# Scores, maxima and exponentials by pairs of heads, and decay factors computed up to four steps ahead, in a decoder layer with a selective scan

## The reference, cut to what matters

```python
# 1: causal attention, 16 heads of 16
scores = einsum('bhqd,bhkd->bhqk', Q, K) / sqrt(16)
attn = softmax(where(causal, scores, -inf), axis=-1)
out = einsum('bhqk,bhkd->bhqd', attn, V)
x = layernorm(x + out.reshape(b, s, 256) @ Wo.T)
# 2: selective scan over ctx, 256 channels, 16 states; x is the gate
def step(state, xs):
    d_t, B_t, C_t, u_t = xs
    dA = exp(d_t[..., None] * A)
    state = state * dA + (d_t * u_t)[..., None] * B_t[:, None, :]
    y_t = einsum('ben,bn->be', state, C_t)
x = layernorm(x + swapaxes((y + D * u) * silu(x), 1, 2))
# 3: mixture of 8 experts, the best 2 for each row
x = layernorm(x + sum_e w_e * (silu(0.5 * x @ w_gate[e]) * (x @ w_up[e]) @ w_down[e] * 0.25))
```

## Time and profile before

| | |
|---|---|
| median of 3 runs | 428.7 us (428.37 to 428.83) |
| the profiled execution | 431.48 us, of which span 429.7 us |
| loop of attention and scan | from about 37 to 238 us |
| busy in the span | PE 79%, DVE 59%, ACT 49%, POOL 58% |

### The profile page before, as it was taken

How to read it: one execution, slowest core, us unless ns; L and a number is a source line. 1 busy time by engine, 2 the same in 40 slices (tenths; PEclk the granted TensorE clock), 3 DMA queues, 4 the chain that set the end, 5 groups by cost and what they waited for, 6 DMA issues and landing times.

```text
span 429.7 us, 5678 instructions
## 1 busy us (share of the span) xinstructions
PE 340.4 (79%) x1780; PEld 205.5 (48%) x1780; DVE 252.1 (59%) x439; ACT 209.9 (49%) x488; POOL 248.5 (58%) x232
## 2 busy tenths in 40 slices
PE   8794868856778677875869586899999999999651
PEld 4352435623446244653435242466666666666441
DVE  2989797974958879688977676112122222222134
ACT  4678786737877678767964100322222222212103
POOL 2075999999978996789888302233233333331214
PEclk9986596965989769896986888999999999999967
DMA  7050110162114510242106950111111111111162
GB/s 209 8 101 3 38 35 31 47 219 50 50 50 82 188 50 26 65 148 84 51 24 218 374 193 0 49 41 46 37 51 49 50 49 37 50 37 38 37 195 99
DMA packets 29455, 34.46 MB, mean 80 GB/s; under 512 B 4074, under 2 KB 23826, under 8 KB 29426
## 3 DMA queue, kind: packets, MB, share of 16 engines
q1 hardware_dynamic: 24770, 26.36, 20.3%
q0 software_dynamic: 2208, 6.03, 4.6%
q10 hardware_dynamic: 2448, 1.71, 1.4%
HBM read 28.92 MB, written 5.18 MB: 79 GB/s over the span
## 4 chain that ended last, share of the span: by engine, by line
PE 36%; DVE 6%; DMA 2%; ACT 2%; POOL 2%; issue 2%; DVEq 0%; POOLq 0%; ACTq 0%
PE psS L1600 18%; PE psD L1619 5%; PE psO L1619 4%; PE psD L1610 2%; PE psS L1450 2%; PE psT L1595 1%; DMA c_rows<-z_out 1%; DVE experts L981 1%; POOL rstd L493 1%; DVE u_sb L1131 1%; PE psT L1379 1%; DMA delta<-x_rows,row_in 1%; DMA z_out<-delta,row_out 1%; PE psT L1444 0%; POOL rstd L492 0%
## 5 line engine op out<-in xcount | busy, mean ns | idle before, releaser
L1600 PE MATMUL psS<-experts,delta 128*128 x184 | 86.5, 593 | 0.5 <-ACT delta L818 0.5
L504 POOL TENSOR_TENSOR experts<-experts,c_rows 128x1024 f32<-128x1024 f32 x31 | 73.0, 2355 | 17.8 <-DVE experts L981 17.4
L981 DVE TENSOR_TENSOR_SCAN experts<-experts,psD 128x512 f32<-128x512 f32 x64 | 74.4, 1204 | 0.0
L572 POOL DMA_INDIRECT z_out<-delta,row_out x23 | 22.8, 991 | 88.4 <-ACT delta L832 88.4
L1379 PE MATMUL psT<-ident,probs_at 128*128 128x128 f32 x192 | 39.2, 340 | 23.4 <-ACT probT L727 23.4
L1205 DVE COPY u_sb<-psD 128x512 f32<-128x512 f32 x23 | 15.9, 692 | 68.7 <-PE psD L1610 68.7
L689 ACT ACTIVATE experts<-delta,A_sb 128x255 f32<-128x255 f32 x128 | 54.7, 517 | 0.5 <-DVE du L929 0.5
L972 DVE TENSOR_TENSOR psD<-du,psD 128x512 f32<-128x512 f32 x64 | 41.6, 688 | 13.2 <-PE psD L1337 12.9
L1600 PEld LDWEIGHTS psS<-experts,delta 128*128 128x128 f32 x184 | 33.1, 190 | 24.3 <-issue 23.3
L1379 PEld LDWEIGHTS psT<-ident,probs_at 128*128 128x128 f32 x192 | 27.4, 172 | 35.1 <-ACT probT L727 33.4
L507 POOL TENSOR_TENSOR experts<-experts 128x512 f32<-128x512 f32 x31 | 40.7, 1312 | 2.4
(11 more groups left out here) (236 smaller groups left out, 591.6 us busy)
## 6 DMA issues: line engine op xcount, KB each, us to landing
c_rows<-c_dram SPq DMA_DIRECT2D x32, 256.0 KB, 3.4
experts<-in_L_ffn_w_gate_dram SPq DMA_DIRECT2D x8, 512.0 KB, 5.9
experts<-in_L_ffn_w_up_dram SPq DMA_DIRECT2D x8, 512.0 KB, 6.9
experts<-in_L_ffn_w_down_dram SPq DMA_DIRECT2D x8, 512.0 KB, 8.1
x_in<-in_x_dram SPq DMA_DIRECT2D x4, 256.0 KB, 5.3
x_rows<-x_sb SPq DMA_DIRECT2D x4, 256.0 KB, 2.5
probs_at<-z_out SPq DMA_DIRECT2D x4, 256.0 KB, 5.1
c_rows<-z_out ACTq DMA_DIRECT2D x4, 256.0 KB, 6.3
```

Of the source, the lines that this page charges most:

```text
L504: pool.tensor_tensor(states[:, g % ST], states[:, g % ST], c_rows[:, g % CR].rearrange("p n (o s) -> p n o s", o=1).broadcast_to([P, 2, HA ...
L981: dve.tensor_tensor_scan(states[:, g % ST, n].rearrange("p h s -> p (h s)"), dA[:, g % DA, n].rearrange("p h s -> p (h s)"), psD[:, n, :], ...
L1600: ins = pe.matmul(psS[:, bank, :], xgT[:, s % 2, k, :], gate_up_of(bass.ds(e, 1), i)[:, k, :], start=(k == 0), stop=(k == FC - 1))
```

## The change

It has three parts; no arithmetic is changed.

1. **Pairs of heads.** `scores(G)` writes mask and scores of heads 0 and 1, then those of heads 2 and 3; each pair waits only for the exponentials that last read its own two banks, and each counts up `score_ps`. `maxima(G, pair)` takes the maxima of two heads, so there are four reductions a group for two. In VectorE's queue pair 0 stands **before** `scan(g)` and pair 1 behind it (before the change only step 0 had its maxima ahead of the scan, and m = 3 had `add_gated` between scan and maxima). The exponentials of a head wait for their own pair.
2. **Decay factors ahead.** The ring of `dA` grows from 3 to 5 (two more tiles of 8 KB a partition, `dA_more`), and `decay` moves to the end of ScalarE's steps, by a table: one at the end of m = 2, 3, 6 and 7, two at the end of m = 4 and 5, none in m = 0 and 1.
3. **Broadcast in m = 5.** Both broadcasts of B stand ahead of the transposes and projections of that step.

The diff, cut:

```diff
-    DA, ST, CR, PR = 3, 5, 4, 8
+    DA, ST, CR, PR = 5, 5, 4, 8
+    SHARED = 3
+    DECAYS_AHEAD = ((), (), (4,), (5,), (6, 7), (8, 9), (10,), (11,))
...
+        def dA(i):
+            return dA_shared[:, i] if i < SHARED else dA_more[:, i - SHARED]
...
             def exponentials(G, r):
-                act.wait_ge(max_rdy, G + 1)
+                act.wait_ge(max_rdy, 2 * G + r // 2 + 1)
...
                 for m in range(NP):
                     g = NP * b + m
-                    if 0 < g < STEPS - 2:
-                        if (g + 2) % NP == 0:
-                            act.wait_ge(du_rdy, (g + 2) // NP + 1)
-                        decay(g + 2)
...
+                    elif g == 1:
+                        decay(3)
...
+                    for ahead in DECAYS_AHEAD[m]:
+                        if NP * b + ahead < STEPS:
+                            if ahead == NP:
+                                act.wait_ge(du_rdy, b + 2)
+                            decay(NP * b + ahead)
...
-            def maxima(G):
-                dve.wait_ge(score_ps, G + 1)
-                dve.tensor_reduce(negmax[:, G % 2, 0], psS[:, :, 0:P], AX_X, ALU.max, negate=True)
-                dve.tensor_reduce(negmax[:, G % 2, 1], psS[:, :, P:SCORE], AX_X, ALU.max, negate=True).then_inc(max_rdy, 1)
+            def maxima(G, pair):
+                heads = slice(2 * pair, 2 * pair + 2)
+                dve.wait_ge(score_ps, 2 * G + pair + 1)
+                dve.tensor_reduce(negmax[:, G % 2, 0, heads], psS[:, heads, 0:P], AX_X, ALU.max, negate=True)
+                dve.tensor_reduce(negmax[:, G % 2, 1, heads], psS[:, heads, P:SCORE], AX_X, ALU.max,
+                                  negate=True).then_inc(max_rdy, 1)
...
                     multiply_b(g)
-                    if g == 0:
-                        maxima(0)
+                    if m < GROUPS:
+                        maxima(GROUPS * b + m, 0)
                     scan(g)
+                    if m < GROUPS:
+                        maxima(GROUPS * b + m, 1)
                     if m == 3 and f >= 0:
                         add_gated(f)
-                    if 0 < m < GROUPS or g > 0 and m == 0:
-                        maxima(GROUPS * b + m)
...
-                for r in range(GH):
+                for pair in ((0, 1), (2, 3)):
                     if g > 0:
 
-                        pe.wait_ge(prob_rdy, GH * (G - 1) + r + 1)
...
+                        pe.wait_ge(prob_rdy, GH * (G - 1) + pair[1] + 1)
...
                     elif m == 5:
-                        if not more:
-                            broadcast_b(g + 1, 0)
-                            broadcast_b(g + 1, 1)
+                        broadcast_b(g + 1, 0)
+                        broadcast_b(g + 1, 1)
                         if f >= 0:
                             transpose_x2(f)
```

34 lines of the change are left out of this document (17 added, 17 removed).

## The result

The changed kernel takes **487.3 us** (median of four runs, 486.4 to 489.1) where the kernel before takes 428.8 (428.4 to 430.0): a ratio of 1.137, 95% interval 1.132 to 1.141. It is slower by 58.5 us. The prediction said slower, 453.5 us, with a range up to 470: the sign was right, the size less than half of what came. The profiled execution took 486.42 us with a span of 484.7.

What follows compares the result with a forecast made beforehand. A ring through TensorE, VectorE and ScalarE sets the pace, no engine being full. Terms 16.4 - 2.5 + 7.5 + 3.4 = 24.8 us on 431.48 give 456.3, less 2.8 for the median: 453.5 us, range 440 to 470.

Steps and rivals of the forecast that it cites:

- The ring: Loop's chain through TensorE, VectorE and ScalarE sets the pace, 7.94 us in m=2; the change brings the scan into it.
- The sum for m=2, 10.0 us: Step m=2 with the scan in the chain: 10.0 us against 7.94; with m=3, +4.1 us a batch, +16.4 in four.
- 10.5 us or more: Sign of being right: take_oT comes this long after take_o of m=4, not 7.7 us.
- The rival that GpSimd sets the loop: GpSimd paces the loop and gets faster as its 12.9 us of waits shrink: 415.8 us, half gain 422; chance 0.07.
- The clock, taken at 3.4 us: TensorE's lower clock in scores and weighing of m=3: 0.85 us four times, +3.4 us; upper bound +15.
- the low clock stays through m=2 and m=3: Rival: TensorE's clock never comes back in these steps, +15 us, 468.5 us; chance 0.15.
- Two heads I take at 1.4, an estimate of a little over half: A pair's scores on TensorE in m=2 at the low clock: 1.4 us, against 2.49 for four heads.
- m=3, taken at 9.9 us: From the scores of m=3 to the turn back of m=4, at the high clock: 9.9 us against 7.93.
- Decays, taken at 7.5 us: Two more decays in m=4 and m=5 delay ScalarE's copy; about 2.5 us reach the next batch, three times: +7.5 us.
- Part 3, for which nothing was taken: Broadcasts of m=5 ahead of projections: TensorE 0.6 us sooner, hidden by the decays; no gain.
- No scan waits for a decay: In the trace before, the waits hold no such row; scans waiting for decay factors after the change were ruled out.
- m=0 and m=1, taken as a gain of 2.5 us: Two steps take 15.7 us; second batch -3.5, first +0.3, last +1.0, together -2.5 us.

Runs made afterwards that it cites:

- scores whole and scan first: Changed kernel with four heads' scores in one piece on TensorE and both pairs' maxima behind the scan: 444.2 us, 1.033 of the kernel before.
- the kernel with fillers: Changed kernel plus products nobody reads, ten behind the scores of m=1 to m=3 and five between the two broadcasts: 469.8 us.
- the pairs alone: Kernel before with part 1 only, scores, maxima and exponentials by pairs, first pair's maxima ahead of the scan: 474.7 us, ratio 1.105.
- the decays alone: Kernel before with part 2 only, decays by the changed table and a ring of five factors: 438.7 us, ratio 1.024.
- the execution of 431.6 us: Profiled execution of the kernel before with part 2 only; its five other executions took 437.8 to 440.9 us.

## Why the prediction was right in kind and too small

**What held.** The ring, and that the scan enters it: VectorE idle ahead of pair 0, broadcasts behind the scans. Against scores whole and scan first, this order alone costs 56.9 us. The sum for m=2, 10.0 us, stands against 9.84 in the kernel with fillers, and there its parts hold too: 5.06 us from the scores to the first transposes (177.42 to 182.48) where they sum to 5.0, and 4.78 from there to the next scores where 4.79 was taken. (The two steps sum to +4.0 us a batch, not +4.1; that is 0.3 us in all.) take_oT came 10.53 us after take_o, "10.5 us or more". The rival that GpSimd sets the loop fell as argued: GpSimd's wait went from 17.4 to 73.3 us.

**The clock, taken at 3.4 us.** This is the largest term that was mis-sized. I held "the low clock stays through m=2 and m=3" for a rival with a chance of 0.15 and +15 us; that is in the main what happened, with a mean granted clock of 0.63 over the two steps. In m=2 of the changed kernel nearly all of the 2.58 us above the forecast lie behind 186.62: 0.83 us to the transposes where 0.4 was taken, and 6.93 from there to the next scores (187.45 to 194.38), where 0.64 + 4.15 was taken. Fillers alone gave 17.5 us back, and didn't raise the clock in the first half of m=1. The rival was too narrow as well: project_out at 225.72 ran 3.78 us at the low level, where its eight products ran 1.89 us in the kernel before. This doesn't come with the ring: with the pairs alone it ran 1.89 us in all three turns, and with scores whole and maxima behind the scan, where there is no such ring, 3.78. It comes with parts 2 and 3. The last stretch grew by 5.26 us: 2.86 between take_o and take_oT by the decays, 1.77 from take_oT to the next scores, where project_out stands, and 0.63 ahead of take_o. The step that failed reads "For the scores and weighing of m=3, which I took at the high clock, I add 0.85 us four times": it costs the clock in one place, with the stage as it was, while the ring with VectorE's scans in it left TensorE waiting for scans in each of m=0 to m=3. In its place the runs show a mean clock of 0.63 through m=2 and m=3, and at least 17.5 us. The Trainium skill's sentence on loops that fall back each time round ("TensorE: Matmul & The Clock Gate", HAM oscillation), cited for the rival, agrees with the rows.

**"Two heads I take at 1.4, an estimate of a little over half".** It measured 2.12 us at the low clock and 1.17 at the high one (177.42 to 178.59 in the kernel with fillers), where 0.85 was taken. The row of four heads' products that I halved was no sum of heads. In the kernel before, the split alone costs 21.5 us; no term of the sum held any of it, since the second pair was left out as hidden. In the changed kernel it is in fact mostly hidden behind the scan, and there the split gives 13.8 us; what the term missed there is 0.1 us in m=2, whose first pair was mostly at the high clock (181.80 to 183.19), and 1.0 us in m=3, whose first pair took 1.88 us (194.38 to 196.26).

**m=3, taken at 9.9 us.** 13.78 after, and 11.69 with fillers. Of the 1.8 us that stay, 0.44 is the first pair's scores (1.29 us up to its maxima, 187.26 to 188.55, where 0.85 was taken) and 0.99 is the wait of the transposes for add_gated, which stands in the ring now that the scan does: an instruction on VectorE behind the scan whose tile TensorE needs. I had listed what waits behind the maxima and left it out. Moving it forward in the changed kernel gained nothing, though (488.0 us), so there it was not what held the loop.

**Decays, taken at 7.5 us.** The term was right for a TensorE at the high clock: the three turns grew by 7.9 us in the trace of the decays alone, and by nothing when the decays stood behind the copies. By the medians it is 8.7 us, in which the execution of 431.6 us counts little. In the changed kernel the turns grew by 13.7 us, and parts 2 and 3 together cost 12.6 on top of the pairs: the late copies, and behind them a project_out that fell to the low clock. TensorE waits 1.61 us for take_x2T at 220.91 there, and four products at 223.22, 1.03 us long before, already take 1.89. Part 3, for which nothing was taken, was never run apart; whether it has a share in this stays open. "No scan waits for a decay", true of the kernel before, was to hold for the changed one as well; it was wrong there in two places, by 0.93 us each.

**m=0 and m=1, taken as a gain of 2.5 us.** They took 17.00 us in the second batch and in the third, where 15.7 was forecast: a gain of 2.2 us in the second (19.17 before) rather than 3.5, and a loss of 1.05 in the third (15.95). The low clock of m=1 is not the reason, since it was there before, with the same rounds of 1.79 us. The pairs are: in m=1 of the third batch VectorE reaches the first pair's maxima 7.26 us after the batch's first scores (172.06), where 5.9 was forecast, and the first copy comes at 12.08 (176.88), where 10.8 was. Of these 1.3 us 0.55 come from m=0 and 0.8 from the pair's scores at the low clock.

In sum, from 450.1 (the forecast without its clock term) to 469.8 (the kernel with fillers) it is 19.7 us; the third batch there takes 62.3 us where 57.6 was forecast, and four such misses of 4.7 make 18.8. Of the 4.7, 2.35 lie in m=0 to m=2, where the fillers themselves cost 1.05, 1.8 in m=3 and 0.7 in the last stretch. Then 17.5 us of clock, where 3.4 was taken.

## What to carry to other kernels

Before an engine's work is split for an earlier hand-over, look whether its pieces ran side by side: a row with twice the products in the same time says that half of them won't take half the time. When a slow instruction enters a ring, ask of every other engine in the ring what it does while it waits; for TensorE, idle time came back here as a lower clock in much of what followed, and at least 17.5 of the 58.5 us were that. And of work moved to a "free" engine, count what is queued behind it at the new place: the same decays, moved out of m=0 and m=1, were worth -2 or +9 us by whether they stood behind the copies of the turn or ahead of them.

## What the runs showed of the hardware

Products of 32 rows each in four groups of rows took the same 0.8 and 1.0 us for two heads and for four, at the low clock, and 0.49 and 0.60 against 0.50 and 0.61 at the high one. And a product that nobody reads can pay: 24 of them in a batch made the kernel before 0.75% faster (mean granted clock 0.92 to 0.93 where it was 0.89 to 0.90), while a different choice of 30 gave no more. And the clock of one engine can hang on another's queue: the changed kernel differs from the pairs alone only by where ScalarE's decays and TensorE's broadcasts of m=5 stand, and the same eight products of project_out ran 3.78 us at a granted clock of 0.50 in the one and 1.89 us at 1.00 in the other.
